# Splitting TensorE's unit of logits and unit of products into interleaved halves in the dispatch phase of a soft mixture of experts

## The reference, cut to what matters

```python
logits = (einsum('tzd,ed->tze', x, phi_w) + phi_b).reshape(t, z, 64, 32)   # 4096 tokens, 2048 slots
D = softmax(logits, axis=3)          # over the 32 slots of one expert
C = softmax(logits, axis=2)          # over the 64 experts
X_tilde = einsum('tznp,tzd->npd', D, x)    # dispatch: 2048 slots x 256 features
...                                        # normalise, tanh, one expert product each
Y = einsum('tznp,npH->tzH', C, Y_tilde)    # combine
```

## Time and profile before

| | us |
|---|---|
| median of three executions (4759.47 to 4761.86) | 4760.71 |
| the profiled execution, its own time | 4761.31 |
| its span, first to last instruction | 4759.6 |
| dispatch f: first logits to the start of the experts phase | 1591.6 to 1972.2 |
| dispatch g: the same | 3946.3 to 4329.8 |

### The profile page before, as it was taken

How to read it: one execution, slowest core, us unless ns; L and a number is a source line. 1 busy time by engine, 2 the same in 40 slices (tenths; PEclk the granted TensorE clock), 3 DMA queues, 4 the chain that set the end, 5 groups by cost and what they waited for, 6 DMA issues and landing times. The chain is left out here.

```text
span 4759.6 us, 96793 instructions
## 1 busy us (share of the span) xinstructions
PE 4417.4 (93%) x39662; PEld 1902.1 (40%) x39662; DVE 4091.2 (86%) x5327; ACT 3128.1 (66%) x5879; POOL 1214.4 (26%) x1206
## 2 busy tenths in 40 slices
PE   7799999999998899899987999999999998998998
PEld 4222222222223565456652222232222245654666
DVE  5899999999986898688848999999998868885887
ACT  3378988789997444344434789888899974443443
POOL 2100001100002577545301000011000015774543
PEclk9699999999999899999997999999999999999999
DMA  6100000000000000300040000000000000004000
GB/s 185 53 22 2 2 15 16 11 15 6 2 2 23 1 1 1 124 20 0 0 134 21 16 2 2 22 9 15 15 2 2 2 22 1 1 1 143 10 13 13
DMA packets 73606, 112.23 MB, mean 24 GB/s; under 512 B 12261, under 2 KB 56629, under 8 KB 68917
## 3 DMA queue, kind: packets, MB, share of 16 engines
q1 hardware_dynamic: 68424, 99.87, 6.3%
q0 software_dynamic: 4768, 6.59, 1.0%
HBM read 73.70 MB, written 31.47 MB: 22 GB/s over the span
## 5 line engine op out<-in xcount | busy, mean ns | idle before, releaser
L851 ACT ACTIVATE a_att_pt<-ps 128x512 f32<-128x512 f32 (+3 forms) x2304 | 1145.2, 561 | 212.1 <-PE ps L783 183.7
L851 ACT ACTIVATE b_att_pt<-ps 128x512 f32<-128x512 f32 (+3 forms) x2304 | 1145.2, 561 | 206.7 <-PE ps L783 178.3
L906 DVE TENSOR_REDUCE a_att_mx<-ps 128x2 f32<-128x1024 f32 (+3 forms) x1040 | 1145.6, 1161 | 87.4 <-PE ps L747 74.7
L906 DVE TENSOR_REDUCE b_att_mx<-ps 128x2 f32<-128x1024 f32 (+3 forms) x1040 | 1145.0, 1161 | 82.3 <-PE ps L747 70.4
L802 PE MATMUL ps<-a_att_pt,a_v 128*17 128x256 f32 (+1 forms) x8704 | 674.6, 382 | 10.7 <-ACT a_att_osb L838 9.8
L802 PE MATMUL ps<-b_att_pt,b_v 128*17 128x256 f32 (+1 forms) x8704 | 670.4, 380 | 10.7 <-ACT b_att_osb L838 9.7
L728 POOL TENSOR_SCALAR_AFFINE_SELECT a_att_pt<-a_att_pt 128x512 f32<-128x512 f32 x128 | 81.6, 637 | 1121.6 <-ACT a_att_pt L851 1109.4
L783 PE MATMUL ps<-a_q,a_k 51*128 51x512 f16 (+3 forms) x1152 | 365.5, 372 | 0.5 <-ACT a_att_pt L851 0.4
L728 POOL TENSOR_SCALAR_AFFINE_SELECT b_att_pt<-b_att_pt 128x512 f32<-128x512 f32 x128 | 81.6, 637 | 1114.5 <-ACT b_att_pt L851 1102.4
L783 PE MATMUL ps<-b_q,b_k 51*128 51x512 f16 (+3 forms) x1152 | 360.7, 368 | 0.2 <-ACT b_att_pt L851 0.2
L747 PE MATMUL ps<-a_k,a_q 48*128 48x512 f16 (+3 forms) x1152 | 299.8, 385 | 47.2 <-DVE a_att_mx L906 37.8
(11 more groups left out here) (330 smaller groups left out, 7206.7 us busy)
## 6 DMA issues: line engine op xcount, KB each, us to landing
f_mix_ct<-in_expert_w SPq DMA_DIRECT2D x64, 256.0 KB, 4.4
g_mix_ct<-in_expert_w SPq DMA_DIRECT2D x64, 256.0 KB, 4.5
a_parts_q<-a_qkv_cut SPq DMA_DIRECT2D x24, 256.0 KB
a_parts_k<-a_qkv_cut SPq DMA_DIRECT2D x24, 256.0 KB
b_parts_q<-b_qkv_cut SPq DMA_DIRECT2D x24, 256.0 KB
b_parts_k<-b_qkv_cut SPq DMA_DIRECT2D x24, 256.0 KB
x<-in_x SPq DMA_DIRECT2D x8, 512.0 KB, 8.7
out<-x SPq DMA_DIRECT2D x8, 512.0 KB, 2.9
```

The source lines that it names most:

```text
L851: act.activation(pt[:, s % PT_RING, i, 0:width], ps[:, at:at + width], ACT.Exp, scale=unscale).then_inc(pt_ready, 1)
L906: dve.tensor_reduce(mx[u % 2][:, h:h + 2, t, c], both, AX.X, ALU.max).then_inc(ring_read, 1)
```

## The change

`logits` and `products` get a second argument b, the half. `logits(n, 0)` waits for the slot and makes the first bank, `logits(n, 1)` makes the second and raises `l_ready`. `products(n, 0)` makes the products of slot blocks 0 to 3, `products(n, 1)` those of blocks 4 to 7, and raises `xa_ready`; both wait for `d_ready` of unit n. The loop of PE alternates them: first bank of logits, first half of products, second bank, second half. No other engine's program changes, nor does any instruction of PE apart from its place.

```diff
-            def logits(n):
+            def logits(n, b):
                 half, t = half_of(n)
-                wait_slot(("L", n))
-                for b in range(UNIT // BANK):
-                    at, e0 = slot(("L", n)) + b * BANK, half * UNIT + b * BANK
-                    for i, (xp, pp, c) in enumerate(TERMS):
-                        mm = pe.matmul(ps[:, at:at + BANK], xlnT[:, xp, c, t * P:(t + 1) * P], phi[:, pp, c, e0:e0 + BANK],
-                                       start=(i == 0), stop=(i == len(TERMS) - 1))
-                mm.then_inc(l_ready, 1)
-
-            def products(n):
+                if b == 0:
+                    wait_slot(("L", n))
+                at, e0 = slot(("L", n)) + b * BANK, half * UNIT + b * BANK
+                for i, (xp, pp, c) in enumerate(TERMS):
+                    mm = pe.matmul(ps[:, at:at + BANK], xlnT[:, xp, c, t * P:(t + 1) * P], phi[:, pp, c, e0:e0 + BANK],
+                                   start=(i == 0), stop=(i == len(TERMS) - 1))
+                if b + 1 == UNIT // BANK:
+                    mm.then_inc(l_ready, 1)
+
+            def products(n, b):
                 half, t = half_of(n)
                 pe.wait_ge(d_ready, n + 1)
-                for eb in range(HALF_EB):
+                for eb in range(HALF_EB // 2 * b, HALF_EB // 2 * (b + 1)):
...
-                mm.then_inc(xa_ready, 1)
+                if b == 1:
+                    mm.then_inc(xa_ready, 1)
...
             for n in range(UNITS_D + LAG):
-                if n < UNITS_D:
-                    logits(n)
-                if n >= LAG:
-                    products(n - LAG)
+                for b in range(2):
+                    if n < UNITS_D:
+                        logits(n, b)
+                    if n >= LAG:
+                        products(n - LAG, b)
                 if n in TURN_AFTER:
                     turn(TURN_AFTER[n])
```

## The result

| | before | after |
|---|---|---|
| median | 4760.1 us | 4948.4 us |
| profiled execution, its own time | 4761.3 | 4946.5 |
| its span | 4759.6 | 4944.8 |
| dispatch f, first logits to end of the last products | 378.3 | 473.0 |
| dispatch g, the same | 380.7 | 472.4 |

One of the four runs of the changed kernel took 7580.6 us at a mean granted clock of 0.849 (the other three had 0.968 and 0.969); it moves the median of 4948.4 a little, and the ratio goes by the other three, 4941.8 to 4950.3, whose median is 4946.5. The ratio after to before is 1.0392, 95% interval 1.0378 to 1.0406: slower by 186 us, where 165 were forecast. In the profiles the two dispatches together are 186 us longer, against 185 for the span; all else is as it was, within 1.2 us.

What follows compares the result with a forecast made beforehand. Dispatch was taken as bound by a loop through several engines; 41.4 + 2.6 + 30.5 = 74.5 us a dispatch, +149 for two, plus 16 for PE's clock, on 4761.3 less 0.6, gave 4926 us, range 4895 to 4965.

Steps and rivals of the forecast that it cites:

- The loop: Dispatch: PE's products and logits plus a 10.85 us chain through DVE, ACT and POOL; 5.36 us a unit becoming 6.73.
- First half: Dispatch, first products to those of unit 31: first two intervals +1.7 us, other 29 gain 1.37 each, sum +41.4.
- Joint: Dispatch, products of unit 31 to 32, waiting for ACT to empty the banks: 9.22 us before, +2.6 forecast.
- Second half: Dispatch, 28 intervals after products of unit 32: 6.85 us a unit, +30.5 us (27 to 38).
- the cuts: POOL's pieces and PE's turns in a dispatch's later 28 intervals: 0.40 us a unit before, mostly fitting into new slack.
- End: Dispatch, the last three products: stand alone as before, 0, within 3 us either way.
- The clock: PE's clock halving after new 3.0 us gaps: 5 falls a dispatch at 1.6 us, +16 us for both dispatches.
- The first rival: PE's clock falls at nearly every gap in dispatch: +253 us, about 5014; chance 0.11.
- No change and faster: Two rivals: PE's own 5.22 us a unit stays the bound, 4761, chance 0.04; halves fill PE's waits, 4735, chance 0.02.

Runs made afterwards that it cites:

- e4: The change with both halves of the products placed between the two banks of logits: 5117.4 us, ratio 1.0747.
- e8: The change with the first logits bank made twice before products of every even unit, and the joined maxima, their pieces, turns and copies left out: 4902.6 us.
- e9: The kernel before with LAG 2 in place of 3, products whole but two units behind: 5185.2 us, ratio 1.0893.
- e2: The change with LAG 4 in place of 3, products four units behind: 4759.5 us, ratio 0.9998.
- e3: The kernel before with LAG 4 in place of 3: 4754.3 us, ratio 0.9989.
- e5: The change with the first bank of logits made a second time ahead of the products of every even unit, same values: 4916.6 us, ratio 1.0323.
- e1: The change with the products' halves moved one half-step back, so the wait stands behind all of a unit's logits again: 4771.0 us, ratio 1.0025.
- e7: The change with the joined maxima, their pieces, turns and copies left out and zeros used in their place: 4917.0 us.

## Why the prediction was right, and by how much off

- **The loop**, three units of 16.07 before and two of 13.46 after: measured 13.47, the alternation 5.22 and 8.25 too. e4, e8 and e9 follow the same formula with other numbers of units and other work, and e2 and e3 fall back to PE's own 5.22, as it says they must.
- **First half**, 41.4: with the gaps filled it is 210.2 - 169.0 = 41.2. The 28 intervals from unit 2 to unit 30 were right, 188.5 us for 188.4; that the sum fits to 0.2 is partly luck. The first two intervals took 15.9 and not the 14.9 forecast, because the bank of logits that starts the chain came cold as well (2.77 for six at 1612.96), for which the prediction took 1.3. The last one took 5.8 and not 6.73, since it is the short one of its pair.
- **Joint**, 2.6: 2.6. Right.
- **Second half**, 30.5 (27 to 38): 34.7 in e5. Of that, 2.5 is the cold pair behind the joint, and 1.3 is fill in the last pair (14.77 for 13.47), which the end gets back. I put the cuts in the new loop at 0.12 us a unit, nearly absorbed; e5 less e8 gives 5.4 / 28 = 0.19. Undersized, inside its bounds.
- **End**, 0 within 3: +4.9, beyond it; 1.6 with the fill. "Stand alone as before" missed that the loop reaches into the end. The products of unit 61 come 10.85 after the last logits of unit 62 in both kernels: 1943.38 to 1954.23 before, 2036.85 to 2047.69 after. What changed is how much of PE's work fits in between, so from unit 60 to 61 it is 8.23 us for 4.50: 3.7 of the 4.9. The other 1.2 is the last burst, cold after (4.33 for 24). The cold burst at 2047.69 cost nothing: from it to the next it is 7.38 us in both kernels.

```profile
1943.38 2.78 PE L1140 MATMUL ps<-f_xtok,area 128*128 128x256 f16 x24
...
1954.23 2.79 PE L1140 MATMUL ps<-f_xtok,area 128*128 128x256 f16 x24 [1.72 <-POOL area L1218]
```

- **The clock**, 5 falls a dispatch at 1.6, 16 us in all: this is the term that was mis-sized. It measured about 30 (14.4 us a dispatch by e5's stretches, 33 us by the ratios). The price of a fall was near (7.2 us for the four of the first half, 1.3 to 2.5 each, 1.8 on average), their number was not: PE's timeline of dispatch f has four in the first half, one at the joint, five in the second half and two at the end, twelve for five, and dispatch g has twelve as well.
- The first rival, a fall at nearly every gap, would have been 5014. It did not happen with gaps of 2.9 us, but it is what e4 did with 4.2. The Trainium skill's rule that a burst after a long wait runs cold (TensorE: Matmul & The Clock Gate, "Loop structure matters more than you think") held in that order, after every gap of 4.18 us in the first half of dispatch f, and only in part in this one, after two of the eleven gaps of 2.87 in the same half.
- No change and faster, together 0.06: out by the loop alone. Waits on PE of 21 us a dispatch looked small because PE's own work nearly filled the loop; its slack was 0.14 us a unit.

Dispatch f lost 94.7 us for 82.5 forecast. The 12.2 between are the clock (14.4 - 8 = 6.4), the second half (34.7 - 30.5 = 4.2) and the end (1.6), by e5's stretches; 2.5 of the second half's 4.2 is one more cold burst, which the fill did not prevent.

## What to carry to other kernels

Where an engine alternates two stages of a software pipeline and a loop through other engines, not its own work, sets the pace, cutting both in halves and interleaving them moves the consumer's wait ahead of the producer's last piece: the loop loses a whole stage of lag for half a stage of work. Before such a change, write down the loop: the work between two uses, the chain through the other engines, and over how many units it closes; here (2.61 + 10.85) / 2 against (5.22 + 10.85) / 3. If halves are wanted, either add a unit of lag (e2) or keep the wait where it was by moving the halves back half a step (e1).

## What was not expected of the hardware

- The same gap of 2.87 us halved PE's clock one time and not the next, in a stretch in which every pair of units does the same work; 4.18 us did so at each gap of the first half of dispatch f (e4). The falls are not scattered at random either: the twelve of dispatch g stand at the same units as those of dispatch f, but for three of the first half, which come one pair later. What picks them was not tested. A kernel with such gaps has a time that depends on how many of them end in a fall: e7's runs spread over 19 us, the longest with the lowest mean clock.
- More work was faster: 1.30 us of repeated matmuls ahead of the products of every even unit, once in each pair, took some 30 us off the launch by holding PEclk at 0.98 in place of 0.95 and 0.94.
